# A hybrid layer on one core: the last two steps of the first attention in another order on ScalarE and VectorE

## The chip, the cores and the metric

The kernel runs on one core of a Trainium2 chip. The metric is the device time of one execution in microseconds; the median of three runs is given. The profile is of one further execution, whose own time stands beside its span below.

## The reference

The input `x` is 4 x 256 tokens of 256 values. Four blocks follow each other, each with a layer norm before it and the residual added behind it:

- the first attention ("a"): 16 heads of size 128, with biases, a causal softmax and an output projection;
- a feed-forward product in int8: each row is scaled to 127 by its largest value, rounded, multiplied by an int8 weight and scaled back;
- the second attention ("b"), cut to its core below;
- the same feed-forward product again.

```python
q, k = _rope(hs @ Wq.T), _rope(hs @ Wk.T)      # _rope: [x1*cos - x2*sin, x2*cos + x1*sin]
s = clip(hs @ Ws1.T @ Ws2.T + bs2, -32, 32)    # 64 slots per head
z = cumlogsumexp(s, over time)
es, enz = exp(s), exp(-z)
A = where(mask, q @ k.T * scale, 0)
ok = enz * (A @ es)
qv = softmax(ok)
W2 = where(mask, (qv * enz) @ es.T, 0)
o = W2 @ v
o_n = o * rsqrt(mean(o * o) + EPS) * g_norm_weight
out = (o_n * g * sigmoid(g)) @ Wo.T
```

## The kernel before

The kernel is one program in which every engine has its own stream of instructions, written out by hand. The engines meet only through semaphores. On each engine the order in the text is the order on the chip: an instruction that waits holds up all behind it on that engine.

**Tiling.** Both attentions work on pairs of heads. There are 8 pairs and two halves of the tokens (two batch elements each), so 16 phases; a phase has two steps, one for each batch element. The first attention has steps 0 to 31, the second again 0 to 31. In a step the kernel works on the attention of one batch element and, on the side, on the projections of the phase ahead. Projections are done in three terms (high by high, high by low, low by high part), of fp32 values split in two.

**The last two steps.** Steps 30 and 31 of the first attention (`x = LAST - 1` and `x = LAST`) are written out, since the phase ahead is the first one of the second attention (its phase 0). Its projections are called tasks: `s` (the slot values), `q0`, `q1`, `k0`, `k1` (queries and keys of the two heads, to be rotated), `z` (running sums of `es`, made by a product with ones), `c0` to `c3` (values and gates of four token tiles) and `et` (transposes of `es`).

**TensorE's order** (L1857 to L1883), which the change leaves alone: transposes of step 30's weights for head 0, `s`, those for head 1, `q0`, the scores of step 31, `q1`, the value product of step 30, `z`, `k0`, the out-projection `out_group`, `k1`; then, for step 31, transposes for head 0, `c0`, transposes for head 1, `c1`, the value product, `c2`, the first scores of the second attention, `et`, the product `b_ok`, `out_group` and `c3`.

**Banks.** In phase 0 the tasks go by turns into two PSUM banks: `s`, `q1`, `k0`, `c0` and `et` into bank 0, and `q0`, `z`, `k1`, `c1` and `c3` into bank 1; `c2` has a third one. A task waits in `b_free` (L1631) until what was in its bank before has been taken out. After a query or a key that means two semaphores: ScalarE's copy and VectorE's cosine product, `b_rotcos`.

**A rotation** has four parts on three engines. ScalarE copies the two halves of the product into `rot_s`, exchanged (two activations, L801 and L802). When both are done, GpSimd multiplies `rot_s` by the sine table (`rope_mul`, L490) and VectorE multiplies the product in PSUM by the cosine table into `rot` (`b_rope_cos`, L1180). VectorE adds the two (`b_rope_add`, L1189). `rot_s` has two parts, one for `q0` and `k0`, one for `q1` and `k1`; so ScalarE's copy of `k0` waits for the sum of `q0`, and that of `k1` for the sum of `q1`.

**The softmax of the first attention.** VectorE adds the mask and takes the row maxima (`a_max_step`, L1106 to L1111), ScalarE takes the exponentials with their row sums (`a_exp_step`, L711), VectorE divides (`a_norm_step`: two small reciprocals at L1116, four scalings at L1120), TensorE transposes, ScalarE copies the transposed weights (`weights_copy`, L730), and TensorE multiplies by the values. ScalarE takes the result out as a high part (`out_copy`, L720), VectorE as a low part (`out_tail`, L1127). `add_group` (L1138) adds the out-projection of a step to the running sum. `b_recip` (L1203) takes reciprocals of the sums that ScalarE's copy of `z` (L808) has left in `zs`; there are four per phase. `b_gate` (L1209) forms the gates of a token tile.

GpSimd's order and SyncE's (all loads are issued there, each behind a semaphore of an earlier phase) are not touched.

Of the kernel before, what the change touches and what calls it, by code (L numbers as in the profile page):

```python
# [74 lines left out]
def layer_kernel(nc, x_in, a_wq, a_bq, a_wk, a_bk, a_wv, a_bv, a_wo, a_bo,  # L75
                 b_wq, b_wk, b_wv, b_wg, b_wo, b_ws1, b_ws2, b_bs2, b_gw,
                 f_w, f_ws, f_bias, consts, out):
    with ExitStack() as ctx:
# [166 lines left out]
        a, b_ = Phase("a_"), Phase("b_")  # L245
# [35 lines left out]
        def slot(phase, j):  # L281

            bank = banks_of(phase)[j]
            before = sum(banks_of(p).count(bank) for p in range(phase))
            return bank, before + banks_of(phase)[:j].count(bank)

        def slot_ps(phase, j):

            return NB * phase + j + 1

        def slot_done(phase, j):

            bank, before = slot(phase, j)
            return bank, before + 1
# [323 lines left out]
        def _(act):  # L618
# [87 lines left out]
            def a_exp_step(x):  # L706
                for h in range(2):

                    act.wait_ge(a_max, 2 * x + h + 1)
                    for r, (lo, hi) in enumerate(((0, P), (P, 3 * P))):  # L710
                        last = s.activation(wt[:, h, lo:hi], wt[:, h, lo:hi], ACT.Exp, bias=negmax[:, h, r:r + 1],  # L711
                                            scale=(1.0, -1.0)[r], accum_out=rowsum[:, h, r:r + 1])
                    last.then_inc(a_exp, 1)

            def out_copy(ph, ready, x):

                act.wait_ge(ready, x + 1)
                src = O_.rearrange("p (h t) -> p h t", h=2)
                half, cols = (x // 2) % 2, slice((x % 2) * T, (x % 2 + 1) * T)
                s.activation(oT_hi[:, half, :, cols], src, ACT.Copy).then_inc(ph.o_hi, 1)  # L720
# [6 lines left out]
            def weights_copy(x, h):  # L727

                act.wait_ge(a_pt_ps, 2 * x + h + 1)
                s.activation(wt2[:, h, :], X_[h][:, 0:384], ACT.Copy).then_inc(a_pt, 1)  # L730
# [50 lines left out]
            def b_task(phase, name):  # L781

                task_j, half = B_TASKS.index(name), phase % 2
                bank, count = slot(phase, task_j)
                done = slot_ps(phase, task_j)
                tl = slice(HT * half, HT * (half + 1))
                if name == "s":

                    act.wait_ge(b_.proj_evac[bank], count + 1)
                    s.activation(es[:, tl, :], clip.rearrange("p (t m) -> p t m", t=HT), ACT.Exp).then_inc(b_es, 1)  # L790

                    act.wait_ge(b_es, phase + 1)
                    s.activation(es_hi[:, :].rearrange("p (t m) -> p t m", t=HT), es[:, tl, :], ACT.Copy).then_inc(b_es_hi, 1)
                elif name[0] in "qk":
                    k = int(name[1])
                    act.wait_ge(b_.proj_ps, done)
                    behind = ROPES.index(name) - 1
                    if phase > 0 or behind >= 1:

                        act.wait_ge(b_rope, 4 * phase + behind)  # L800
                    s.activation(rot_s[0:M, k, :], PJ[bank][M:P, :], ACT.Copy)  # L801
                    s.activation(rot_s[M:P, k, :], PJ[bank][0:M, :], ACT.Copy).then_inc(b_.proj_evac[bank], 1)  # L802
                elif name == "z":
                    act.wait_ge(b_.proj_ps, done)
                    if phase > 0:

                        act.wait_ge(b_recip_done, HT * phase)
                    s.activation(zs[:, :], PJ[bank], ACT.Copy).then_inc(b_.proj_evac[bank], 1)  # L808
                elif name == "et":
                    act.wait_ge(b_.proj_ps, done)  # L810
                    s.activation(esT[:, half * HALF:(half + 1) * HALF], PJ[bank], ACT.Copy).then_inc(b_.proj_evac[bank], 1)
                else:


                    k = int(name[1])
                    act.wait_ge(b_.proj_ps, done)
                    if phase > 0 or k >= 2:

                        other, count = slot_done(phase - (k < 2), B_TASKS.index("c%d" % ((k + 2) % 4)))
                        act.wait_ge(b_.proj_evac[other], count)  # L820
                    s.activation(v[:, HT * half + k, :], PJ[bank][:, 0:2 * P], ACT.Copy)
                    s.activation(gt[:, k % 2, :], PJ[bank][:, 2 * P:4 * P], ACT.Tanh, scale=0.5).then_inc(b_gt, 1)
# [106 lines left out]
            x = LAST - 1  # L929
# [3 lines left out]
            weights_copy(x, 1)  # L933
            b_task(0, "s")
            b_task(0, "q0")
            a_exp_step(x + 1)
            b_task(0, "q1")
            out_copy(a, a.o_ps, x)
            b_task(0, "z")
            b_task(0, "k0")  # L940
            x = LAST
            weights_copy(x, 0)
            b_task(0, "k1")
            weights_copy(x, 1)
            b_task(0, "c0")
            a_out_weights(PHASES - 1)
# [15 lines left out]
        def _(dve):  # L962
# [150 lines left out]
            def a_norm_step(x):  # L1113
                for h in range(2):
                    dve.wait_ge(a_exp, 2 * x + h + 1)
                    d.reciprocal(rinv[:, h, :], rowsum[:, h, :]).then_inc(a_rinv, 1)  # L1116
                for h in range(2):
                    dve.wait_ge(a_rinv, 2 * x + h + 1)
                    for r, (lo, hi) in enumerate(((0, P), (P, 3 * P))):
                        ins = d.tensor_scalar(wt[:, h, lo:hi], wt[:, h, lo:hi], rinv[:, h, r:r + 1], None, ALU.mult)  # L1120
                    ins.then_inc(a_norm, 1)

            def out_tail(ph, x):

                half, cols = (x // 2) % 2, slice((x % 2) * T, (x % 2 + 1) * T)
                dve.wait_ge(ph.o_hi, x + 1)
                d.tensor_tensor(oT_lo[:, half, :, cols], O_.rearrange("p (h t) -> p h t", h=2),  # L1127
                                oT_hi[:, half, :, cols].bitcast(F32), ALU.subtract).then_inc(ph.o_lo, 1)
# [45 lines left out]
            def b_rope_cos(phase, name):  # L1174

                j, k, m = B_TASKS.index(name), int(name[1]), "qk".index(name[0])
                bank, count = slot_done(phase, j)
                dve.wait_ge(b_.proj_evac[bank], count)
                col = (K_QCOS, K_COS)[m]
                d.tensor_tensor(rot[:, k, :].rearrange("p (b t) -> p b t", b=2), PJ[bank].rearrange("p (b t) -> p b t", b=2),  # L1180
                                const[:, col:col + T].unsqueeze(1).to_broadcast([P, 2, T]), ALU.mult).then_inc(b_rotcos, 1)

            def b_rope_add(phase, name):

                k, m, half = int(name[1]), "qk".index(name[0]), phase % 2
                count = 4 * phase + ROPES.index(name) + 1
                dve.wait_ge(b_rotcos, count)
                dve.wait_ge(b_rotmul, count)
                d.tensor_tensor((qT, kT)[m][:, k, half * HALF:(half + 1) * HALF], rot[:, k, :], rot_s[:, k, :],  # L1189
                                ALU.add).then_inc(b_rope, 1)  # L1190
# [7 lines left out]
            def b_recip(phase, k):  # L1198

                bank, count = slot_done(phase, B_TASKS.index("z"))  # L1200
                if k == 0:
                    dve.wait_ge(b_.proj_evac[bank], count)
                d.reciprocal(enz[:, HT * (phase % 2) + k, :], zs[:, k * P:(k + 1) * P]).then_inc(b_recip_done, 1)  # L1203

            def b_gate(phase, k):

                bank = slot(phase, B_TASKS.index("c%d" % k))[0]
                dve.wait_ge(b_gt, HT * phase + k + 1)
                d.scalar_tensor_tensor(out=G[:, HT * (phase % 2) + k, :], in0=gt[:, k % 2, :], scalar=1.0,  # L1209
                                       in1=PJ[bank][:, 2 * P:4 * P], op0=ALU.add, op1=ALU.mult  # L1210
                                       ).then_inc(b_.proj_evac[bank], 1)
# [127 lines left out]
            x = LAST - 1  # L1339
# [2 lines left out]
            b_rope_cos(0, "q0")  # L1342
            a_max_step(x + 1)
            b_rope_cos(0, "q1")
            b_rope_add(0, "q0")
            a_norm_step(x + 1)
            out_tail(a, x)
            b_recip(0, 0)
            b_rope_add(0, "q1")
            b_rope_cos(0, "k0")  # L1350
            add_group(a, x)
            b_recip(0, 1)
            x = LAST
            b_rope_cos(0, "k1")
            b_rope_add(0, "k0")
            b_rope_add(0, "k1")
            b_gate(0, 0)
            b_gate(0, 1)
            out_tail(a, x)
# [576 lines left out]
```

## Time and profile before

| | us |
|---|---|
| median of three runs | 793.27 (792.58 to 793.73) |
| the profiled execution, its own time | 789.8 |
| its span, first to last instruction | 788.0 |
| TensorE busy | 756.8 (96%) |
| VectorE busy | 584.4 (74%) |
| ScalarE busy | 488.3 (62%) |
| GpSimd busy | 386.7 (49%) |

In the profile PE is TensorE, DVE is VectorE, ACT is ScalarE, POOL is GpSimd and SP is SyncE. All times are counted from the span's start. The first attention fills about the first 320 us, and the stretch that the change touches lies between 298 and 322 us.

### The profile page before, as it was taken

To read this page: it belongs to the slowest core of one execution; us is meant where nothing else is said; L and a number is where in the kernel's file an instruction comes from. 1 tells how busy PE (TensorE), PEld (TensorE's weight loads), DVE (VectorE), ACT (ScalarE), POOL (GpSimd) and SP (SyncE) were. 2 spreads that over 40 slices of the span, in tenths; PEclk is the share of its full clock that TensorE was granted. 3 is DMA by queue.
4 is the path that set the end of the run, shared out by engine and by line. 5 is a ranking of instruction groups with operands and counts; after the bars stand their busy time and mean duration, and the time that the engine had idled before them with its cause. 6 is when DMAs were issued, how large, how long until landed. Compare 5 with 4: busy or idle time off the path is not lost.

```text
span 788.0 us, 13104 instructions
## 1 busy us (share of the span) xinstructions
PE 756.8 (96%) x4482; PEld 643.2 (82%) x4482; DVE 584.4 (74%) x1470; ACT 488.3 (62%) x1283; POOL 386.7 (49%) x368
## 2 busy tenths in 40 slices
PE   8999999999999998999999999999999999999964
PEld 6888888888878886888888888888888878788853
DVE  4655456556656656698999898879898997988864
ACT  4755676656766676656767666665667677566520
POOL 4533224223334524556665766655566566766321
PEclk9999999999999999999999999999999999999996
DMA  7222111211111122202111111120211112010100
GB/s 244 76 66 87 54 54 56 66 54 54 54 54 55 54 67 67 68 15 67 54 41 41 54 47 35 54 68 14 68 54 40 42 54 67 15 55 13 41 1 28
DMA packets 43894, 43.40 MB, mean 55 GB/s; under 512 B 4098, under 2 KB 43522, under 8 KB 43700
## 3 DMA queue, kind: packets, MB, share of 16 engines
q1 hardware_dynamic: 43828, 42.55, 17.3%
q8 instruction: 37, 0.61, 0.3%
q14 instruction: 29, 0.24, 0.1%
HBM read 41.49 MB, written 1.05 MB: 54 GB/s over the span
## 4 chain that ended last, share of the span: by engine, by line
PE 84%; DVE 8%; ACT 5%; issue 2%; DMA 1%; POOL 0%; SPq 0%; POOLq 0%; ACTq 0%; DVEq 0%
PE ps L1493 22%; PE ps L1682 10%; PE ps L1569 7%; PE ps L1500 5%; PE ps L1526 5%; PE ps L1574 3%; PE ps L1696 3%; PE ps L1551 3%; PE ps L1534 3%; PE ps L1723 2%; PE ps L1709 2%; PE ps L1745 2%; PE ps L1744 2%; PE ps L1743 2%; PE ps L1697 2%
## 5 line engine op out<-in xcount | busy, mean ns | idle before, releaser
L418 POOL TENSOR_TENSOR w_lo<-w_raw,w_hi 128x512 fp32r<-128x512 f32 x64 | 81.4, 1285 | 74.1 <-ACT w_hi L634 73.3
L1493 PE MATMUL ps<-xT_hi,w_hi 128*128 128x512 f32 x256 | 109.1, 426 | 3.9 <-ACT rot_s L802 2.8
L1493 PE MATMUL ps<-xT_hi,w_lo 128*128 128x512 f32 x256 | 100.4, 392 | 0.0
L1493 PE MATMUL ps<-xT_lo,w_hi 128*128 128x512 f32 x256 | 100.2, 391 | 0.0
L490 POOL TENSOR_TENSOR rot_s<-rot_s,const 128x512 f32<-128x512 f32 x64 | 81.7, 1286 | 21.6 <-ACT rot_s L802 21.6
L1215 DVE TENSOR_TENSOR wt<-ps,const 128x384 f32<-128x384 f32 x128 | 68.1, 554 | 25.6 <-PE ps L1726 11.5
L418 POOL TENSOR_TENSOR wc_lo<-wv,wc_hi 128x512 fp32r<-128x512 f32 x16 | 20.4, 1277 | 104.0 <-ACT wc_hi L634 104.0
L1099 DVE TENSOR_TENSOR v<-ps,bv_b 128x256 f32<-128x256 f32 x64 | 27.0, 423 | 53.1 <-PE ps L1500 53.1
L711 ACT ACTIVATE wt<-wt,negmax 128x128 f32<-128x128 f32 (+1 forms) x128 | 56.7, 444 | 15.5 <-DVE negmax L1111 15.5
L1203 DVE RECIPROCAL enz<-zs 128x128 f32<-128x128 f32 x64 | 60.4, 943 | 0.0
L1493 PEld LDWEIGHTS ps<-xT_hi,w_hi 128*128 128x128 f32 x256 | 48.2, 188 | 14.3 <-ACT rot_s L802 3.1
L1493 PEld LDWEIGHTS ps<-xT_hi,w_lo 128*128 128x128 f32 x256 | 48.1, 188 | 11.0
L512 POOL TENSOR_TENSOR qp<-oke,enz 128x256 f32<-128x256 f32 x32 | 23.6, 739 | 67.9 <-ACT oke L826 67.9
L1682 PE MATMUL ps<-wc_hi,xT_hi 128*128 128x512 f32 x128 | 55.9, 437 | 0.9 <-issue 0.8
L1180 DVE TENSOR_TENSOR rot<-ps,const 128x512 f32<-128x512 f32 x64 | 43.6, 682 | 15.5 <-ACT rot_s L802 15.5
L720 ACT ACTIVATE oT_hi<-ps 128x512 fp32r<-128x512 f32 x62 | 36.5, 588 | 29.7 <-PE ps L1762 29.0
L418 POOL TENSOR_TENSOR wc_lo<-wc,wc_hi 128x1024 fp32r<-128x1024 f32 x16 | 38.2, 2386 | 34.0 <-ACT wc_hi L634 34.0
L1493 PEld LDWEIGHTS ps<-xT_lo,w_hi 128*128 128x128 f32 x256 | 48.4, 189 | 6.8
L1682 PE MATMUL ps<-wc_hi,xT_lo 128*128 128x512 f32 x128 | 50.4, 394 | 0.0
L1682 PE MATMUL ps<-wc_lo,xT_hi 128*128 128x512 f32 x128 | 50.2, 392 | 0.0
L1569 PE MATMUL ps<-oT_hi,wo_hi 128*128 128x512 f32 x124 | 49.9, 403 | 0.0
L730 ACT ACTIVATE wt<-ps 128x384 f32<-128x384 f32 x64 | 29.7, 487 | 32.1 <-PE ps L1534 32.0
(177 smaller groups left out, 2328.4 us busy)
## 6 DMA issues: line engine op xcount, KB each, us to landing
w_raw<-a_w_q SPq DMA_DIRECT2D x16, 256.0 KB, 3.0
w_raw<-a_w_k SPq DMA_DIRECT2D x16, 256.0 KB, 3.8
wv<-a_w_v SPq DMA_DIRECT2D x16, 256.0 KB, 2.7
wo<-a_w_o SPq DMA_DIRECT2D x16, 256.0 KB, 2.7
w_raw<-b_Wq SPq DMA_DIRECT2D x16, 256.0 KB, 2.7
w_raw<-b_Wk SPq DMA_DIRECT2D x16, 256.0 KB, 3.2
wc<-b_Wv SPq DMA_DIRECT2D x16, 256.0 KB, 2.7
wc<-b_Wg SPq DMA_DIRECT2D x16, 256.0 KB, 3.0
```

The lines of the kernel that those rows point to most:

```text
L418: g.tensor_tensor(lo[:, :, :], raw[:, :, :], hi[:, :, :].bitcast(F32), ALU.subtract).then_inc(ph.w_lo, 1)
L490: g.tensor_tensor(ap, ap, const[:, col:col + T].unsqueeze(1).to_broadcast([P, 2, T]), ALU.mult).then_inc(b_rotmul, 1)
L711: last = s.activation(wt[:, h, lo:hi], wt[:, h, lo:hi], ACT.Exp, bias=negmax[:, h, r:r + 1], scale=(1.0, -1.0)[r], accum_out=rowsum[:, h, ...
L720: s.activation(oT_hi[:, half, :, cols], src, ACT.Copy).then_inc(ph.o_hi, 1)
L1180: d.tensor_tensor(rot[:, k, :].rearrange("p (b t) -> p b t", b=2), PJ[bank].rearrange("p (b t) -> p b t", b=2), const[:, col:col + T].unsq ...
L1203: d.reciprocal(enz[:, HT * (phase % 2) + k, :], zs[:, k * P:(k + 1) * P]).then_inc(b_recip_done, 1)
L1215: d.tensor_tensor(dst, src[:, 0:384], tri3, ALU.mult).then_inc(done, 1)
L1493: ins = mm(PJ[bank], w[:, m, c, h * P:(h + 1) * P], x[:, c, cols], start=(t == 0), stop=(t == len(terms) - 1))
L1500: ins = mm(bank_ap, x[:, c, cols], w[:, c, :], start=(t == 0), stop=(t == len(terms) - 1))
L1526: ins = mm(W_[h][:, lo:hi], qT[:, h, t0 + r * P:t0 + (r + 1) * P], kT[:, h, t0:t0 + hi - lo], start=True, stop=True)
L1569: mm(Y_, w[:, h, c * P:(c + 1) * P], oT_hi[:, half, h, :], start=(h == 0 and w is wo_hi), stop=False)
L1682: ins = mm(PJ[bank], x[:, c, tile], w[:, c, :], start=(c == 0 and t == 0), stop=(c == C - 1 and t == 2))
```

## The change

ScalarE, step 30: the exponentials of step 31 (`a_exp_step(x + 1)`) stood between `q0` and `q1`; they now stand behind `q1`, the high part of step 30's result (`out_copy`) and `z`. ScalarE's copy of `k1` stood behind the first copy of step 31's transposed weights; it now stands ahead of it, right behind that of `k0`.

VectorE, steps 30 and 31: the low part of step 30's result (`out_tail`) and the first reciprocal (`b_recip(0, 0)`) stood behind the normalising (`a_norm_step`); `out_tail` now stands ahead of the sum of `q0`, and the reciprocal behind that sum, both ahead of the normalising. The sum of `q1` stood ahead of the cosine product of `k0`; it now stands behind that and behind `add_group`. The second reciprocal (`b_recip(0, 1)`) moves behind the sums of `k0` and `k1`.

No instruction is added or taken away, and TensorE's, GpSimd's and SyncE's orders are the same.

```diff
@@ ScalarE
             b_task(0, "s")
             b_task(0, "q0")
-            a_exp_step(x + 1)
             b_task(0, "q1")
             out_copy(a, a.o_ps, x)
             b_task(0, "z")
+            a_exp_step(x + 1)
             b_task(0, "k0")
+            b_task(0, "k1")
             x = LAST
             weights_copy(x, 0)
-            b_task(0, "k1")
             weights_copy(x, 1)
@@ VectorE
             b_rope_cos(0, "q0")
             a_max_step(x + 1)
             b_rope_cos(0, "q1")
+            out_tail(a, x)
             b_rope_add(0, "q0")
+            b_recip(0, 0)
             a_norm_step(x + 1)
-            out_tail(a, x)
-            b_recip(0, 0)
-            b_rope_add(0, "q1")
             b_rope_cos(0, "k0")
             add_group(a, x)
-            b_recip(0, 1)
+            b_rope_add(0, "q1")
             x = LAST
             b_rope_cos(0, "k1")
             b_rope_add(0, "k0")
             b_rope_add(0, "k1")
+            b_recip(0, 1)
             b_gate(0, 0)
             b_gate(0, 1)
```

## Rows read from the trace of the kernel before

**Rows 1.** The page's first part: busy time, share, instructions.

```profile
PE 756.8 (96%) x4482; PEld 643.2 (82%) x4482; DVE 584.4 (74%) x1470; ACT 488.3 (62%) x1283; POOL 386.7 (49%) x368
```

**Rows 2.** The waits of TensorE over the whole span: total us, times, longest.

```profile
PE ps L1493 <- ACT rot_s L802: 2.8, 1, 2.8
...
PE ps L1682 <- issue: 0.8, 1, 0.8
```

**Rows 3.** The chain that ended last, in order of time: start, us, what.

```profile
304.26 1.86 ACT wt L711 x8
```

**Rows 4.** TensorE's timeline: start, us, line, tiles, count, [idle before, releaser].

```profile
302.95 0.40 PE L1493 MATMUL ps<-xT_hi,w_lo 128*128 128x512 f32 x1
...
305.07 0.28 PE L1663 MATMUL ps<-es_lo,sums 128*128 128x256 f32 x1
308.17 0.47 PE L1493 MATMUL ps<-xT_hi,w_hi 128*128 128x512 f32 x1 [2.81 <-ACT rot_s L802]
...
309.63 0.39 PE L1569 MATMUL ps<-oT_hi,wo_hi 128*128 128x512 f32 x1
...
310.99 0.39 PE L1493 MATMUL ps<-xT_hi,w_hi 128*128 128x512 f32 x1
...
312.35 0.49 PE L1534 MATMUL ps<-const,wt 128*128 128x128 f32 x3
313.65 0.47 PE L1682 MATMUL ps<-wc_hi,xT_hi 128*128 128x512 f32 x1 [0.81 <-issue]
...
315.69 0.47 PE L1682 MATMUL ps<-wc_hi,xT_hi 128*128 128x512 f32 x1
...
319.85 0.59 PE L1696 MATMUL ps<-qT,kT 128*128 128x256 f32 x2
```

**Rows 5.** ScalarE's timeline of the same stretch.

```profile
306.15 0.59 ACT L801 ACTIVATE rot_s<-ps 64x512 f32<-64x512 f32 x1
306.75 0.59 ACT L802 ACTIVATE rot_s<-ps 64x512 f32<-64x512 f32 x1
307.37 0.60 ACT L720 ACTIVATE oT_hi<-ps 128x512 fp32r<-128x512 f32 x1
307.86 0.59 ACT L808 ACTIVATE zs<-ps 128x512 f32<-128x512 f32 x1
...
321.80 0.60 ACT L811 ACTIVATE esT<-ps 128x512 f32<-128x512 f32 x1 [0.94 <-PE ps L1668]
```

**Rows 6.** VectorE's timeline of the same stretch.

```profile
304.68 0.28 DVE L1111 TENSOR_REDUCE negmax<-wt 128x1 f32<-128x128 f32 x1
307.37 0.69 DVE L1180 TENSOR_TENSOR rot<-ps,const 128x512 f32<-128x512 f32 x1 [2.41 <-ACT rot_s L802]
307.98 1.27 DVE L1189 TENSOR_TENSOR qT<-rot,rot_s 128x512 f32<-128x512 f32 x1
309.17 0.21 DVE L1116 RECIPROCAL rinv<-rowsum 128x2 f32<-128x2 f32 x2
309.36 1.01 DVE L1120 TENSOR_SCALAR wt<-wt,rinv 128x128 f32<-128x128 f32 x4
...
310.88 0.94 DVE L1203 RECIPROCAL enz<-zs 128x128 f32<-128x128 f32 x1
...
312.87 0.68 DVE L1180 TENSOR_TENSOR rot<-ps,const 128x512 f32<-128x512 f32 x1
...
320.71 1.21 DVE L1215 TENSOR_TENSOR wt<-ps,const 128x384 f32<-128x384 f32 x2 [0.72 <-PE ps L1697]
```

**Rows 7.** GpSimd's timeline of the same stretch.

```profile
307.42 1.28 POOL L490 TENSOR_TENSOR rot_s<-rot_s,const 128x512 f32<-128x512 f32 x1 [2.50 <-ACT rot_s L802]
```

**Rows 8.** The instructions of L1120 and of L1189, whole span: ns min/median/max.

```profile
L1120 DVE TENSOR_SCALAR wt<-wt,rinv x128: 266/343/2174, 22.1 to 310.0; 128x128 f32<-128x128 f32 x64, 128x256 f32<-128x256 f32 x64
...
L1189 DVE TENSOR_TENSOR qT<-rot,rot_s x32: 621/684/1434, 308.0 to 730.2; 128x512 f32<-128x512 f32 x32
```

**Rows 9.** Busy us of each engine (count), a stretch of the second attention.

```profile
400.00:500.00 100.00, 98.23 (x609) 83.11 (x608) 89.26 (x184) 67.52 (x177) 65.86 (x62) 1.00 0.16 48
```

## The prediction

> **What bounds the kernel now.** I read the busy shares first: TensorE is busy 96% of the span [rows 1], so a change elsewhere is worth something only where TensorE stands still. Next the list of TensorE's waits: two of them belong to the stretch that the change touches: 2.8 us for ScalarE's half swap `rot_s` and 0.8 us put down to "issue" [rows 2]. Then the chain that ended last: at 304.26 it leaves TensorE and runs through ScalarE's softmax exponentials for 1.86 us [rows 3]. Last the timelines of that stretch, engine by engine, to see who holds whom.
>
> The first wait is read from four of them. `q1`'s product ends at 302.95+0.40 = 303.35 and its bank must be emptied before `k0` may start in it. ScalarE, though, has the exponentials of step 31 next in its order, waits for their row maxima, runs them until 304.26+1.86 = 306.12, and only then swaps `q1`'s halves (306.15 to 307.34) [rows 3, 5]. VectorE's cosine product follows (307.37 to 308.06) [rows 6], and `k0` starts at 308.17, 2.81 us after the slot sum's product `z` ended at 305.35 [rows 4]. So TensorE, with nothing else to do, waits for a softmax that it needs only at 312.35 [rows 4].
> The second wait, called "issue", is a semaphore after all: `c0` goes into `k0`'s bank and needs VectorE's cosine product of `k0`. That stands behind the normalising, the copy of the low part, a reciprocal and a rotation sum, runs 312.87 to 313.55 [rows 6], and `c0` starts at 313.65 [rows 4]: 0.10 us after, the same step as 308.06 to 308.17.
>
> **The change part by part.** No instruction, transfer or byte is added or removed; SyncE's and GpSimd's orders stay as they are, so no DMA issue changes its place in a queue. Only orders on ScalarE and VectorE change, and the sum is a new schedule of 303 to 318 us, worked out with the durations of before. All before `q1`'s swap keeps its time.
>
> (a) *ScalarE: `q1`, `out_copy` and `z` ahead of the exponentials.* The swap takes 306.15 to 307.34, that is 1.19 us [rows 5]. It now starts when the product is done, 303.39, and ends at 304.58. `out_copy` (0.60 [rows 5]) follows behind the value product, which stands ahead of `z` on TensorE and so is over by about 304.7; it ends by 305.3. The `z` copy (0.59 [rows 5]) starts at `z`'s end, 305.39, to 305.98. ScalarE starts a next activation 0.49 us after the last (307.37 to 307.86 [rows 5]), so the exponentials run 305.88 to 307.75: 1.6 us later than before. That is the price of this part.
>
> (b) *VectorE: the cosine product of `q1`.* The maxima end at 304.68+0.28 = 304.96 [rows 6], so it is they that are late next, not the swap; engines here begin about 0.08 ahead of the last one's end, so 304.88 to 305.57. `k0` can start at 305.68 and not at 308.17: 2.49 us gained, with 0.33 us of the wait left.
>
> (c) *TensorE up to `c0`.* The pitches are as before: `k0` to the out-projection 309.63-308.17 = 1.46, this to `k1` 1.36, `k1` to the transposes of step 31 1.36 [rows 4]. So 307.14, 308.50 and 309.86 for the transposes. They need the normalised weights: the two small reciprocals start at 307.78 once the exponentials are over, 0.19 us later the four scalings, 1.01 us long [rows 6], to about 308.95. The later softmax is hidden by 0.9 us at the transposes. Without that cover each microsecond more would be lost at `c0`, up to the bound under (d).
> Ahead of them VectorE has the low part of step 30 (0.69, a form like the cosine product, 305.49 to 306.17), the sum of `q0` (306.08 to about 306.8) and the reciprocal 0.94 us long [rows 6] (to 307.63): these fill the time of the exponentials, and cost nothing up to 307.75.
>
> (d) *The keys.* ScalarE swaps `k0` after the exponentials, 307.77 to 308.95 (its product ends at 305.68+1.62 = 307.30). VectorE's cosine product follows, 308.98 to 309.66. `c0` is thus free to go right behind the first transposes, at about 310.1 or, if their 0.49 us [rows 4] are all to pass first, 310.35. The second wait is gone: `c0` comes 3.3 to 3.5 us earlier.
> What is late next is `c1`, which needs bank 1 back from `k1`. ScalarE's swap of `k1` waits for the sum of `q1`, since both use one half of `rot_s`; and that sum now stands behind the normalising, `k0`'s cosine product and the group sum, which is of the cosine product's size (0.68 [rows 6]): 308.98+0.68, then the group sum 309.58 to 310.25, then the sum from 310.17. GpSimd's product for `k0` runs then, 309.03 to 310.32 (0.08 us after the swap, 1.28 us long [rows 7]).
>
> What such a meeting costs is in the rows: the sum at 307.98 took 1.27 us, and ended 0.55 us after GpSimd's product 307.42 to 308.70 [rows 6, 7], where the median is 0.684 and the longest 1.434 [rows 8]. So the sum of `q1` ends at 310.87 (0.55 after GpSimd, or 0.70 after its own start: the same here). The ends are 0.62 and 1.43 us [rows 8], 310.79 to 311.60; I take 310.87, by the row of the nearest overlap. The swap of `k1` is 310.92 to 312.12, its cosine product 312.15 to 312.84, `c1` starts at 312.94.
> The Trainium skill, "SBUF — State Buffer", section "Who interferes with whom", says that a VectorE instruction with both inputs in SBUF contends with a GpSimd instruction that reads SBUF, and whoever issues first makes the other wait out the whole instruction. By that rule, the trace agrees: 1.27 us where 0.684 is usual. It also speaks against the new order, as the third case below.
>
> (e) *Behind `c1`.* Before, `c1` started at 315.69 [rows 4]; the gain there is 315.69-312.94 = 2.75 us. From there TensorE runs through, before and after: the copies of the weights of step 31, which ScalarE now does after `k1`'s swap, two activations at the pitch of 0.49 us behind 312.12, end at about 313.1, ahead of the value product (312.94+1.46 = 314.4). The sums of the keys end at about 314.65: the first 0.55 behind GpSimd's product for `k1` (312.20+1.28 = 313.48), the second 0.6 later. The first scores, at 319.85 before [rows 4] and 317.10 now, need them: 2.4 us to spare. `recip(0,1)` (0.94) now falls between them and the gates, and the gate of `c0`, over by about 316, is needed only by the transposes behind those scores. VectorE was idle 0.72 us before the first score masks, and ScalarE 0.94 us before `esT` [rows 5, 6]; both reach them early again. So all engines enter the second attention as they did, 2.75 us earlier.
>
> **The sum.** -2.75 us. The profiled execution took 789.8 us for a span of 788.0 and would take about 787.05; the median of the three runs is 793.27 (792.58 to 793.73), 3.5 us above it. I carry the difference over: 793.27-2.75 = 790.5.
>
> **The rivals.**
> *More comes off.* If `c1` need not wait for the swap of `k1`, only TensorE's own order counts: `c0` 310.35, the transposes 1.46 later, 0.49 for them, `c1` at 312.30: 3.39 us, 789.9. For it: the sum of `q1` might miss GpSimd; against: the swap and the cosine product behind it (1.87 us) are plain work. It decides if that sum ends 0.64 us earlier.
> *The normalising meets GpSimd.* The scalings are over at 308.95, and GpSimd starts on `k0` at 309.03: they miss each other by 0.1 us. If the last scaling is caught, it ends about 0.28 after GpSimd (310.6), `k0`'s cosine product at 311.2, the group sum at 311.8, the sum of `q1` at 312.4, and `c1` starts 2.07 later at 314.48: a gain of 1.21, 792.1. A scaling has taken 2.174 us where the median is 0.343 [rows 8]; that speaks for it. Against: swap and scalings both hang on the end of the exponentials, and 1.19+0.08 is longer than 0.19+1.01. The lock rule of the Trainium skill's page named above is the mechanism of this case.
> *Given back in the second attention.* There VectorE is busy 89.26 of 100 us [rows 9]; if it set the pace, an earlier start would end in a wait, and the time is 793.3. Against: TensorE is busy 98.23 in the same stretch [rows 9], and nothing there hangs on the clock on the wall.
> *Slower.* GpSimd's two products (for `q1` and `k0`) fall on VectorE between the exponentials and the sum of `q1`, and each catches a scaling at its worst (2.174-0.343 = 1.83 each), and the sum too (1.434-0.684 = 0.75): 4.41 us on the path to `c1`. From 2.75 on the change loses; at 4.41 it is 794.9. For it: the key's swap is now chained behind more VectorE work than before. Against: GpSimd's product for `q1` is over by 306.2, before any scaling.
>
> **How the numbers follow.** From no change a measurement of this kernel can tell about 0.2%, 1.6 us. The forecast has 0.62, more 0.10, the meeting 0.12, given back 0.10, slower 0.06. Faster by over 0.2%: forecast and more, less a little for scatter, 0.70; within: the meeting, given back and that scatter, 0.23; slower 0.07. The range reaches from the largest gain with the runs' scatter, 793.27-3.39-0.6 = 789.3, past the meeting with the same scatter to 792.8, and leaves out most of the last two.
>
> **What would show it.** `k0` about 0.3 us behind `z` and led by VectorE's maxima; no wait at `c0`; a wait of 0.6 to 0.9 us at `c1`; a rotation sum of `q1` that ends near GpSimd's product; first scores 2.7 us earlier and the same distance from there to the end. A wait over 1.5 us at `c1`, or at step 31's transposes, would make the size wrong; an unchanged end with earlier scores, the reason.

## The result, and the profile after

| | before | after |
|---|---|---|
| median of six runs, us | 792.61 (792.11 to 793.73) | 788.12 (786.79 to 790.07) |
| ratio of after to before | | 0.994, 95% interval 0.993 to 0.995 |
| the profiled execution, its own time, us | 789.8 | 789.05 |
| its span, us | 788.0 | 787.3 |

The kernel became 4.5 us faster, where 2.75 were forecast; the time lies below the range. The two profiled executions differ by 0.75 us only. This contradiction is what the experiments are about.

First TensorE's timeline of the changed kernel (start, us, line, tiles, idle before and its releaser), the rows that answer to [rows 4]:

```profile
306.37 0.28 PE L1663 MATMUL ps<-es_lo,sums 128*128 128x256 f32 x1
306.96 0.47 PE L1493 MATMUL ps<-xT_hi,w_hi 128*128 128x512 f32 x1 [0.31 <-issue]
...
308.42 0.40 PE L1569 MATMUL ps<-oT_hi,wo_hi 128*128 128x512 f32 x1
...
309.80 0.39 PE L1493 MATMUL ps<-xT_hi,w_hi 128*128 128x512 f32 x1
...
311.16 0.49 PE L1534 MATMUL ps<-const,wt 128*128 128x128 f32 x3
311.41 0.48 PE L1682 MATMUL ps<-wc_hi,xT_hi 128*128 128x512 f32 x1
...
314.34 0.47 PE L1682 MATMUL ps<-wc_hi,xT_hi 128*128 128x512 f32 x1 [0.97 <-DVE rot L1180]
...
318.50 0.59 PE L1696 MATMUL ps<-qT,kT 128*128 128x256 f32 x2
```

The last product of `z` starts at 306.37, and at 305.07 before: this execution is 1.30 us late, nearly all of it from its first 20 us on. (Over the first 15 us its granted clock was 0.89 on average, and 1.00 in the trace of before.) Counted against `z`, that is with 1.30 taken off, the schedule came out as worked out:

| start, us | before | forecast | after, less 1.30 |
|---|---|---|---|
| `k0` | 308.17 | 305.68 | 305.66 |
| `k1` | 310.99 | 308.50 | 308.50 |
| transposes of step 31 | 312.35 | 309.86 | 309.86 |
| `c0` | 313.65 | about 310.1 | 310.11 |
| `c1` | 315.69 | 312.94 | 313.04 |
| first scores | 319.85 | 317.10 | 317.20 |

ScalarE's timeline, for [rows 5]:

```profile
304.68 0.59 ACT L801 ACTIVATE rot_s<-ps 64x512 f32<-64x512 f32 x1 [0.61 <-PE ps L1493]
...
306.69 0.60 ACT L808 ACTIVATE zs<-ps 128x512 f32<-128x512 f32 x1
307.18 0.39 ACT L711 ACTIVATE wt<-wt,negmax 128x128 f32<-128x128 f32 x1
...
309.06 0.60 ACT L801 ACTIVATE rot_s<-ps 64x512 f32<-64x512 f32 x1
...
312.28 0.59 ACT L801 ACTIVATE rot_s<-ps 64x512 f32<-64x512 f32 x1 [2.02 <-DVE qT L1189]
```

Ahead of the swap of `q1` ScalarE stands still for 0.61 us, for the product and no longer for the softmax; the exponentials follow `z`; and ahead of the swap of `k1` ScalarE stands for 2.02 us until VectorE has the sum of `q1`. That sum is in VectorE's timeline, for [rows 6]:

```profile
305.98 0.28 DVE L1111 TENSOR_REDUCE negmax<-wt 128x1 f32<-128x128 f32 x1
306.17 0.68 DVE L1180 TENSOR_TENSOR rot<-ps,const 128x512 f32<-128x512 f32 x1
...
309.15 0.99 DVE L1120 TENSOR_SCALAR wt<-wt,rinv 128x128 f32<-128x128 f32 x4
310.29 0.69 DVE L1180 TENSOR_TENSOR rot<-ps,const 128x512 f32<-128x512 f32 x1
...
311.49 0.69 DVE L1189 TENSOR_TENSOR qT<-rot,rot_s 128x512 f32<-128x512 f32 x1
313.50 0.69 DVE L1180 TENSOR_TENSOR rot<-ps,const 128x512 f32<-128x512 f32 x1 [1.32 <-ACT rot_s L802]
```

and GpSimd's product for `k0` beside it, for [rows 7]:

```profile
310.33 1.30 POOL L490 TENSOR_TENSOR rot_s<-rot_s,const 128x512 f32<-128x512 f32 x1 [2.85 <-ACT rot_s L802]
```

The maxima end at 306.26 and the cosine product of `q1` follows them; the scalings end at 310.14, 0.19 us ahead of GpSimd's start; the sum of `q1` ends at 312.18, 0.55 us behind GpSimd's end at 311.63. So the traces hold a gain of 2.65 us between `z` and the first scores. The medians hold 4.5. The remaining 1.9 us are not in these two traces. The 0.75 us between the two profiled executions are the 2.65 less those 1.30 at the start and 0.6 at the end, by which the changed kernel's execution was the longer one.

### The profile page after: what moved, and what is told of

Read it like the earlier page. It is cut to its first block, busy times and chain, and to the rows that moved or that the text cites. A ratio compares the mean times of both kernels' runs of the same rounds, so it can differ in the third digit from the quotient of the medians.

```text
span 787.3 us, 13104 instructions
## 1 busy us (share of the span) xinstructions
PE 758.0 (96%) x4482; PEld 644.5 (82%) x4482; DVE 583.7 (74%) x1470; ACT 487.7 (62%) x1283; POOL 386.5 (49%) x368
## 4 chain that ended last, share of the span: by engine, by line
PE 84%; DVE 8%; ACT 4%; issue 2%; DMA 1%; POOL 0%; SPq 0%; POOLq 0%; ACTq 0%; DVEq 0%
PE ps L1493 22%; PE ps L1682 10%; PE ps L1569 7%; PE ps L1526 5%; PE ps L1500 5%; PE ps L1574 3%; PE ps L1551 3%; PE ps L1696 3%; PE ps L1534 2%; PE ps L1723 2%; PE ps L1709 2%; PE ps L1552 2%; PE ps L1745 2%; PE ps L1744 2%; PE ps L1743 2%
## 5 line engine op out<-in xcount | busy, mean ns | idle before, releaser
L1215 DVE TENSOR_TENSOR wt<-ps,const 128x384 f32<-128x384 f32 x128 | 68.1, 554 | 25.7 <-PE ps L1726 11.6
L1569 PE MATMUL ps<-oT_hi,wo_lo 128*128 128x512 f32 x124 | 48.6, 392 | 0.0
```

The source lines that it names most:

```text
L1215: d.tensor_tensor(dst, src[:, 0:384], tri3, ALU.mult).then_inc(done, 1)
L1569: mm(Y_, w[:, h, c * P:(c + 1) * P], oT_hi[:, half, h, :], start=(h == 0 and w is wo_hi), stop=False)
```

## The experiments

Two theories of the 1.9 us stood at first. A: start and end of an execution fall differently each time. B: the change gains at a second place. A third, C, came out of the first run.

**The kernel before, once more.** No edit.

> The kernel before, word for word, timed against itself. Theory A (the change is worth what its schedule shows, 2.65 us at c1 in the traces, and the rest of the 4.5 us in the medians lies in how the start and the end of an execution fall, which differ from execution to execution): difference 0 within about 1 us, and a trace that against the first one of before differs only ahead of 15 us and behind 765 us, by 1 to 2 us. Theory B (the change gains 1.9 us more at another place, every time): difference 0 too, but start and end the same as in the first trace within 0.3 us.

Measured: ratio 1.0 (0.9991 to 1.0009), a median of 792.4 us, so nothing drifts. But the trace is neither that of A nor that of B. Its windows (us; busy us and count of TensorE, its weight loads, VectorE, ScalarE and GpSimd; then TensorE's granted clock, DMA share, GB/s) are these:

```profile
306.40:309.10 2.70, 0.00 (x0) 0.00 (x0) 0.73 (x2) 2.64 (x8) 0.69 (x1) 1.00 0.00 2
309.16:309.90 0.74, 0.74 (x3) 0.64 (x4) 0.74 (x1) 0.29 (x1) 0.54 (x1) 1.00 0.00 0
309.93:313.20 3.27, 3.27 (x9) 2.55 (x8) 3.27 (x10) 1.19 (x2) 0.57 (x1) 0.51 0.00 0
313.57:316.60 3.03, 3.03 (x16) 2.49 (x15) 1.84 (x3) 1.09 (x2) 0.94 (x1) 1.00 0.00 0
```

and some of TensorE's rows:

```profile
306.07 0.28 PE L1663 MATMUL ps<-es_lo,sums 128*128 128x256 f32 x1
309.16 0.47 PE L1493 MATMUL ps<-xT_hi,w_hi 128*128 128x512 f32 x1 [2.81 <-ACT rot_s L802]
309.47 0.40 PE L1493 MATMUL ps<-xT_lo,w_hi 128*128 128x512 f32 x1
309.70 0.39 PE L1493 MATMUL ps<-xT_hi,w_lo 128*128 128x512 f32 x1
...
310.27 0.63 PE L1493 MATMUL ps<-xT_lo,w_hi 128*128 128x512 f32 x1
310.69 0.63 PE L1493 MATMUL ps<-xT_hi,w_lo 128*128 128x512 f32 x1
...
312.40 0.63 PE L1569 MATMUL ps<-oT_hi,wo_lo 128*128 128x512 f32 x1
...
313.57 0.39 PE L1493 MATMUL ps<-xT_hi,w_hi 128*128 128x512 f32 x1
...
318.06 0.47 PE L1682 MATMUL ps<-wc_hi,xT_hi 128*128 128x512 f32 x1 [0.90 <-DVE rot L1180]
```

`z` ends at 306.35, TensorE waits 2.81 us as in [rows 4], and `k0` starts at full clock. 0.8 us later products of 512 columns start 0.42 us apart and not 0.23 (310.27 to 310.69): the granted clock is 0.51, its level of 1.2 GHz, until about 313.4, and then 1.00 again. Measured against `z` (0.28 of 306.07 to 305.07: 1.00 us), `c1` comes at 317.06 and not at 315.69: 1.4 us later. In the first trace of before the clock stayed at 1.00 through this stretch. That gave theory C: in most executions of the kernel before the wait costs its own length and a fall of the clock behind it, and the trace on which the forecast rests shows one of the few without it.

**The changed kernel, once more.** No edit.

> The changed kernel, word for word, again. Theory A: a median 2 to 4 us below before, not the same figure as the first time, with the traces 2.65 us apart between 20 and 760 us and the remainder ahead of 15 us and behind 765 us. Theory B: 4.5 us below before again, with a trace in which 1.9 us more have gone at the same place.

Measured: 787.48 us against 792.43, ratio 0.9943 (0.993 to 0.9956): the gain repeats, 5.0 us. The trace has `c1` 2.65 us earlier against `z` (0.37 us late here), as the first one, and the granted clock is 1.00 from 304 to 318 us.

```profile
305.44 0.28 PE L1663 MATMUL ps<-es_lo,sums 128*128 128x256 f32 x1
...
313.41 0.47 PE L1682 MATMUL ps<-wc_hi,xT_hi 128*128 128x512 f32 x1 [0.96 <-DVE rot L1180]
```

Theory A falls, since the excess comes back; B falls too, since no second place shows: from the first scores to VectorE's last score masks (L1215), which is nearly the whole second attention, all traces of this document take 441.0 to 441.2 us.

**The wait filled.** TensorE works through the wait, for nothing: `keep_busy` issues eleven products into PSUM bank 7, which nobody reads.

```diff
             b_task(0, "z")
+            pe.wait_ge(a.y_acc, x - 1)
+            keep_busy(7, oT_hi[:, 0, 0, :], 11)
             b_task(0, "k0")
```

> The kernel before, with 11 products of 512 columns that nobody uses on TensorE between z and k0, about 2.6 us that fit into the wait of 2.81 us. Theory C (the typical execution of before loses more than its first traced one showed: after that wait the granted clock falls to half for some 3 us, and the first scores come 1.4 us later): the granted clock stays at 1.00 from 305 to 316 us, k0 starts where it did, and the median falls by 1.2 to 1.6 us although no useful instruction has moved. Rival (the missing 1.9 us lie in start and end, and the fall is a matter of chance with no share in the medians): within 0.5 us of before.

Measured: 790.08 us against 792.27, ratio 0.9974 (0.9963 to 0.9984). That is 2.2 us, or 1.3 to 2.9 by the interval. TensorE's rows, and the window behind the wait:

```profile
305.67 0.28 PE L1663 MATMUL ps<-es_lo,sums 128*128 128x256 f32 x1
305.78 2.68 PE L1386 MATMUL ps<-oT_hi 128*128 128x512 f32 x11
308.78 0.47 PE L1493 MATMUL ps<-xT_hi,w_hi 128*128 128x512 f32 x1 [0.32 <-issue]
...
310.01 0.39 PE L1493 MATMUL ps<-xT_hi,w_lo 128*128 128x512 f32 x1
...
314.26 0.47 PE L1682 MATMUL ps<-wc_hi,xT_hi 128*128 128x512 f32 x1 [0.80 <-issue]
...
316.30 0.47 PE L1682 MATMUL ps<-wc_hi,xT_hi 128*128 128x512 f32 x1
```

```profile
308.78:313.20 4.42, 4.42 (x21) 3.64 (x21) 4.42 (x10) 1.46 (x3) 1.84 (x2) 1.00 0.00 0
```

The eleven products fill 305.78 to 308.46. `k0` (308.78, less 0.60 for the later `z`: 308.18) and `c1` (315.70) start where they did in the first trace of before, and the clock is 1.00. `k0`, `c1` and the first scores start no earlier than in that trace (14.79 us from `z` to the first scores, and 14.78 there), and the median is still 2.2 us below that of before. This is the missing part by itself. (The traced execution, 791.75 us, is the slowest of the eight: its end took 1.4 us longer than that of the first trace of before.) The changed kernel at 787.48 and 788.12 (in other series of runs) is a further 2.0 to 2.6 us below this one, where its schedule is worth 2.65 by the traces. The gain of 2.2 is above the 1.2 to 1.6 that I expected from the one trace with the fall, but 1.3 to 1.6 lies within its interval.

**The wait put back into the changed kernel.** TensorE waits ahead of `k0` for the exponentials:

```diff
             b_task(0, "z")
+            pe.wait_ge(a_exp, 2 * LAST + 2)
             b_task(0, "k0")
```

> The changed kernel, with TensorE made to wait ahead of k0 until the exponentials of step 31 are over: a wait of about 2.5 us again, with all else in the new order. By the schedule alone k0 comes 2.2 us later and c1, which had a wait of 1 us to spare, about 1.7 us later than in the changed kernel. Theory C: the clock falls to half behind the wait in most executions, and the median is 2.6 to 3.1 us above that of the changed kernel. Rival: 1.7 us above it, the clock at 1.00.

Measured: 790.77 us, 3.3 above the changed kernel (787.48, on another chip) and 0.9977 (0.9968 to 0.9986) of before. The traced execution:

```profile
305.26 0.28 PE L1663 MATMUL ps<-es_lo,sums 128*128 128x256 f32 x1
307.97 0.50 PE L1493 MATMUL ps<-xT_hi,w_hi 128*128 128x512 f32 x1 [2.43 <-ACT wt L711]
...
314.94 0.47 PE L1682 MATMUL ps<-wc_hi,xT_hi 128*128 128x512 f32 x1 [0.53 <-DVE rot L1180]
```

Here the wait is 2.43 us and the clock stays at 1.00; `c1` (314.94, less 0.19) comes 1.7 us later than in the changed kernel, as by the schedule alone. The twelve runs split: six at 791.1 to 792.1 us with a mean granted clock of 0.988, six at 789.2 to 790.4 us with 0.989 to 0.992. The upper six fit C, the lower six the schedule; the upper ones' traces were not taken, so this is support and not proof.

**VectorE's new order alone.** In the changed kernel ScalarE's part is undone:

```diff
             b_task(0, "q0")
+            a_exp_step(x + 1)
             b_task(0, "q1")
             out_copy(a, a.o_ps, x)
             b_task(0, "z")
-            a_exp_step(x + 1)
             b_task(0, "k0")
-            b_task(0, "k1")
             x = LAST
             weights_copy(x, 0)
+            b_task(0, "k1")
```

> VectorE's new order with ScalarE's old one. The exponentials still stand ahead of q1's swap, so the wait of 2.81 us stays, and with it, by theory C, the fall of the clock. The cosine product of k0 comes earlier, so c0 no longer waits, but the sum of q1 and the swap of k1 then hold c1: 0 to 0.4 us earlier than before, and a median within 0.6 us of before. Rival (each half brings its own share, ScalarE's 3.2 of the 5 us): 1.8 us faster.

Measured: 792.55 us, ratio 1.0003 (0.9994 to 1.0013): nothing, as expected. The wait of 2.81 us is in its trace, and behind it

```profile
309.70:313.10 3.40, 3.40 (x10) 2.67 (x8) 2.89 (x9) 1.18 (x2) 0.58 (x1) 0.51 0.00 0
```

the clock is at 0.51 again. This is the second trace with the fall. TensorE's rows:

```profile
305.83 0.28 PE L1663 MATMUL ps<-es_lo,sums 128*128 128x256 f32 x1
308.92 0.47 PE L1493 MATMUL ps<-xT_hi,w_hi 128*128 128x512 f32 x1 [2.81 <-ACT rot_s L802]
...
317.80 0.47 PE L1682 MATMUL ps<-wc_hi,xT_hi 128*128 128x512 f32 x1 [0.88 <-DVE rot L1180]
```

`c1` starts at 317.04 against `z` (0.76 us late), and at 317.06 in the trace of before with the fall: VectorE's order moves nothing there.

**ScalarE's new order alone.** In the changed kernel VectorE's part is undone:

```diff
             b_rope_cos(0, "q1")
-            out_tail(a, x)
             b_rope_add(0, "q0")
-            b_recip(0, 0)
             a_norm_step(x + 1)
+            out_tail(a, x)
+            b_recip(0, 0)
+            b_rope_add(0, "q1")
             b_rope_cos(0, "k0")
             add_group(a, x)
-            b_rope_add(0, "q1")
+            b_recip(0, 1)
             x = LAST
...
             b_rope_add(0, "k1")
-            b_recip(0, 1)
```

> ScalarE's new order with VectorE's old one. My schedule: k0 starts 2.5 us earlier (the first wait is gone), but VectorE's old order puts the low part, the reciprocal of 0.94 us and the sum of q1 ahead of k0's cosine product, so c0 waits 1.4 us more than its turn and c1 starts about 1.85 us earlier than before. Rival (all the gain comes from ScalarE's order alone): c1 2.65 us earlier, as in the changed kernel.

Measured: 789.27 us against 792.43, ratio 0.996 (0.9948 to 0.9972), 3.2 us.

```profile
305.81 0.28 PE L1663 MATMUL ps<-es_lo,sums 128*128 128x256 f32 x1
...
312.33 0.47 PE L1682 MATMUL ps<-wc_hi,xT_hi 128*128 128x512 f32 x1 [1.27 <-issue]
...
314.38 0.47 PE L1682 MATMUL ps<-wc_hi,xT_hi 128*128 128x512 f32 x1
```

Against `z` (0.74 us late here) `c1` starts at 313.64: 2.05 us earlier than before, where I had worked out 1.85; `c0` waits 1.27 us for its cosine product, and the clock stays at 1.00 behind that shorter wait. 2.05 and the 1.4 of the fall make 3.4. So ScalarE's part removes the long wait, and no fall stands in its trace; VectorE's, worth nothing alone, adds 0.6 us on top by the traces (1.8 by the medians, 789.27 and 787.48, of five and six runs).

**The sum of `q1` early.** In the changed kernel on VectorE:

```diff
             b_rope_add(0, "q0")
-            b_recip(0, 0)
+            b_rope_add(0, "q1")
             a_norm_step(x + 1)
             b_rope_cos(0, "k0")
             add_group(a, x)
-            b_rope_add(0, "q1")
+            b_recip(0, 0)
```

> The changed kernel with the sum of q1 right behind that of q0, and the first reciprocal in its place behind the group sum. If what is late at c1 is the sum of q1, on which ScalarE's swap of k1 waits, the swap starts when k1's product ends, about 0.9 us earlier, and c1 comes 0.8 to 0.95 us earlier than in the changed kernel, 3.5 us earlier than before; the wait of 0.97 us at c1 falls to 0.1 or less. Rival (the wait at c1 comes from VectorE or ScalarE being full there): c1 within 0.2 us of the changed kernel.

Measured: 786.28 us against 792.43, ratio 0.9931 (0.9917 to 0.9944).

```profile
305.62 0.28 PE L1663 MATMUL ps<-es_lo,sums 128*128 128x256 f32 x1
...
310.61 0.48 PE L1682 MATMUL ps<-wc_hi,xT_hi 128*128 128x512 f32 x1
...
312.63 0.47 PE L1682 MATMUL ps<-wc_hi,xT_hi 128*128 128x512 f32 x1
```

Against `z` (0.55 us late) `c1` starts at 312.08, 0.96 us earlier than in the changed kernel, and the wait there is gone. What was late at `c1` was the sum of `q1`, behind which the swap of `k1` had to stand. The median is 1.2 us below the changed kernel's of the same series; the runs of the two overlap (785.75 to 788.11, and 786.84 to 789.0), so the trace shows the gain better than the times do.

**And the cosine product of `q1` between the maxima of the two heads.** Against the kernel just above; `a_max_step` now takes the heads that it is to treat:

```diff
             b_rope_cos(0, "q0")
-            a_max_step(x + 1)
+            a_max_step(x + 1, (0,))
             b_rope_cos(0, "q1")
+            a_max_step(x + 1, (1,))
```

> The kernel with the early sum of q1, and besides the cosine product of q1 between the maxima of the two heads. What is left of the first wait (0.31 us, led by the maxima) should fall to about 0.04 us, k0 and all behind it 0.27 us earlier, with the second head's maxima still ahead of its exponentials: c1 3.85 us earlier than in the first trace of before. In the medians 0.27 us more than with the early sum alone, which the runs may not resolve. Rival: the maxima of the second head come late for the exponentials, and c1 is where it was or later.

Measured: 786.83 us against 792.27, ratio 0.9928 (0.9916 to 0.994).

```profile
305.70 0.28 PE L1664 MATMUL ps<-es_lo,sums 128*128 128x256 f32 x1
306.03 0.47 PE L1494 MATMUL ps<-xT_hi,w_hi 128*128 128x512 f32 x1
...
312.49 0.47 PE L1683 MATMUL ps<-wc_hi,xT_hi 128*128 128x512 f32 x1
```

`k0` starts 0.05 us behind `z`, and `c1` at 311.86 against `z` (0.63 us late), 3.83 us ahead of the first trace of before. The runs do not tell this version from the one above.

**The swap of `k1` in its old place.** In the changed kernel on ScalarE, read by its trace alone:

```diff
             b_task(0, "k0")
-            b_task(0, "k1")
             x = LAST
             weights_copy(x, 0)
+            b_task(0, "k1")
             weights_copy(x, 1)
```

> The changed kernel with ScalarE's swap of k1 back in its old place, behind the first copy of step 31's weights; read by its trace alone. In the changed kernel ScalarE waits 2.02 us ahead of that swap for the sum of q1, and the copy (0.49 us) can run in that wait, since the transposes that it needs end 0.6 us before the swap: c1 within 0.1 us of the changed kernel against z, so this move is worth nothing by itself. Rival: the copy ends after the sum of q1 and c1 comes 0.4 us later.

Measured, in one run: `c1` at 313.28 with `z` 0.23 us late, so 313.05, and 313.04 in the changed kernel. That move brought nothing: ScalarE's wait for the sum of `q1` hides the copy.

## Why the prediction was wrong

- **(a) to (e), the schedule: right.** Each start came within 0.1 us, the two places named as late next (VectorE's maxima at `k0`, the sum of `q1` at `c1`) were the late ones, and the wait at `c1` was 0.97 us where 0.6 to 0.9 was said. In (d) the sum of `q1` did end 0.55 us behind GpSimd's product, but it overlapped that by 0.14 us only (311.49 to 311.63) and took 0.69, as long as any other. "0.55 after GpSimd" and "0.70 after its own start" give the same end, so whether GpSimd held it up at all can't be told here.
- **The sum: wrong.** "I carry the difference over" failed. The profiled execution of before lay 3.5 us below the median, and I took this for an offset that both kernels share. In part it was the thing itself: that execution was one without the fall of the clock. Against the second trace of before, whose span is 2.6 us longer, 1.4 of it are the fall and 1.0 an early start (see the table below).
- **What the runs' mean clock says.** Of the 26 runs of before in the last series 22 have a mean granted clock of 0.985 to 0.988, four 0.990 or 0.992; the first traced one had 0.992. The eight runs with the wait filled have 0.990 to 0.993. This fits a fall in most executions of before, but does not place it: the mean holds start and end of a run too, where the clock also falls, differently in each trace. (In the second trace of before the windows 10 to 15 and 770 to 775 us have 0.69 and 0.66; the traced run of the kernel with the product between the maxima has a mean of 0.988 and the clock at 1.00 in this stretch.) That most executions of before have the fall rests on two of three traces and on the median of the filled kernel.
- **Step (b) was mis-sized by it: this is the step that failed.** The wait of 2.81 us was priced by its length, and what it does to the products behind it was put at nothing, without a reason. What it cost in the usual run was that and the slow products behind it: 1.4 us at `c1` in the traces with the fall, 2.2 us (1.3 to 2.9) in the runs. Taken out: 2.65 of schedule and 1.4 to 2.2 of clock make 4.0 to 4.9, and 4.5 (4.0 to 5.5) and 5.0 (3.5 to 5.5) were measured.
- **The range** ended at 789.3, since its lower end was the largest gain that the schedule could give. No rival was about the clock, although the chain had a long standstill of TensorE in it.
- **The rivals.** The meeting with GpSimd did not come about (0.19 us apart), nothing was given back in the second attention, and "more comes off" is a fact only of the two later versions, where the sum of `q1` is early.

The traced executions, cut into four stretches, show where the kernels differ:

| us | before | before, 2nd trace | wait filled | changed | changed, 2nd trace |
|---|---|---|---|---|---|
| start to `z` | 305.07 | 306.07 | 305.67 | 306.37 | 305.44 |
| `z` to the first scores | 14.78 | 16.16 | 14.79 | 12.13 | 12.13 |
| first scores to the last score masks | 441.13 | 441.17 | 441.11 | 441.14 | 440.99 |
| from there to the end | 27.03 | 27.16 | 28.39 | 27.61 | 28.39 |

Only the second row goes with the edits, and it holds 4.0 us between the trace of before with the fall and the changed kernel. Start and end differ by up to 1.4 us between these traces, and by up to 1.0 between two of the same kernel. What stays open is whether the fall costs more than its 1.4 us of the traces: the 2.2 of the runs has an interval of 1.3 to 2.9, so it need not, and only one or two executions of each kernel were traced.

## What to carry to other kernels

A trace is one execution: where its own time lies outside the runs' range, as 789.8 did below 792.11 to 793.73, look for what it lacks before a sum is carried over to the median. A wait of TensorE is to be priced by its length and by the clock behind it; filling it with idle work, as here, tells the two apart. And when an order changes on one engine, the other's is worth redoing: VectorE's new order alone brought nothing, and behind ScalarE's it did.

## What the runs showed of the hardware

The granted clock fell to 0.51 (of 2.4 GHz) behind a wait of TensorE of 2.81 us in two of three traces with that wait, 0.7 to 0.8 us after work had begun again (309.93 to 313.20 in the first window shown, and 1.00 from 313.57), while TensorE was busy throughout. It did not fall behind waits of 2.43 and 1.27 us in the one trace of each. The Trainium skill, "TensorE: Matmul & The Clock Gate", section "HAM oscillation — how this bites in real kernels", says that a kernel in which TensorE waits between two pieces of work can start the second one at half the clock. The traces agree that the second piece loses the clock, with products 0.42 us apart where 0.23 is usual (309.47 to 309.70, 310.27 to 310.69), though not from its start: its first 0.74 us had 1.00. The kernel here lost by it although TensorE is busy 96% of the span.
